# Moving the early scatters of a one-core decoder layer between the last steps of batches 14 and 15

## The reference

```python
x = layernorm(x + linear_attention(x))            # q softmax over 16 features, k softmax over tokens
x = layernorm(x + cross_attention(x, ctx, ctx))   # 16 heads of 16, scores 128x128 per head
probs = softmax(gelu(x @ wg1 + bg1) @ wg2)        # 8 experts per token
top_vals, top_idx = top_k(probs, 2)
h = gelu(einsum('nd,edh->enh', x, w_in))          # 512 hidden
o = einsum('enh,ehd->end', h, w_out)
x = layernorm(x + einsum('ne,end->nd', gates, o)) # gates: zero but for the two best
```

## Time and profile before

| what | value |
|---|---|
| median of 3 executions | 425.79 us (424.82 to 425.82) |
| the profiled execution, its own time | 424.05 us |
| its span, first to last instruction | 422.3 us |
| PE busy | 344.7 us, 82% |
| DVE busy | 308.2 us, 73% |
| ACT busy | 221.9 us, 53% |
| POOL busy | 218.0 us, 52% |

### The profile page before, as it was taken

One profiled execution on the slowest core, in us unless ns is written; L12 is line 12 of the kernel. 1 busy time (PEld: TensorE's weight loads), 2 busy tenths in 40 slices (PEclk: granted clock), 3 DMA queues, 4 the chain that ended last, 5 costly groups with the idle time before them and its releaser, 6 DMA issues. The chain is left out here.

```text
span 422.3 us, 12354 instructions
## 1 busy us (share of the span) xinstructions
PE 344.7 (82%) x4025; PEld 279.1 (66%) x4025; DVE 308.2 (73%) x912; ACT 221.9 (53%) x518; POOL 218.0 (52%) x287
## 2 busy tenths in 40 slices
PE   2977999999999999999888664688999999999100
PEld 1656777877778687776766343576899999988100
DVE  2866989888888888888887737378777655655193
ACT  3425666676766766667765236263545444343044
POOL 8344456765757657576547762633223333422173
PEclk9998999999999999999999885589999999999755
DMA  7610222210222112220012221416434322221493
GB/s 223 223 36 1 78 76 77 76 57 23 77 76 79 40 39 76 78 77 23 32 52 75 81 78 47 157 52 191 142 104 127 90 75 68 88 64 40 148 362 125
DMA packets 21387, 38.35 MB, mean 91 GB/s; under 512 B 3696, under 2 KB 11120, under 8 KB 21328
## 3 DMA queue, kind: packets, MB, share of 16 engines
q1 hardware_dynamic: 16768, 26.06, 19.7%
q0 software_dynamic: 3408, 9.41, 6.2%
q10 hardware_dynamic: 1152, 2.10, 1.3%
HBM read 24.71 MB, written 12.84 MB: 89 GB/s over the span
## 5 line engine op out<-in xcount | busy, mean ns | idle before, releaser
L586 POOL DMA_INDIRECT parts<-QKT,rows_all x39 | 37.6, 964 | 76.8 <-DVE QKT L1220 70.4
L328 PE MATMUL bank<-QS,EW 128*128 128x256 f16 (+1 forms) x384 | 61.7, 262 | 4.0 <-DVE XB L1033 2.6
L492 POOL TENSOR_TENSOR rstd<-veps,neghalf 128x1 f32<-128x1 f32 x48 | 38.7, 806 | 38.5 <-DVE veps L856 38.1
L1396 PE MATMUL bank<-EW,QV 128*128 x312 | 48.6, 273 | 1.4 <-DVE R L1212 0.5
L1212 DVE TENSOR_TENSOR R<-scratch,QV 128x512 f16<-128x512 f32 x39 | 26.8, 691 | 30.1 <-ACT scratch L776 18.4
L328 PE MATMUL bank<-XB,EW 128*128 128x256 f16 (+1 forms) x192 | 48.5, 261 | 0.0
L776 ACT ACTIVATE scratch<-bank 128x512 f32<-128x512 f32 x39 | 23.4, 600 | 39.2 <-PE bank L328 39.1
L328 PEld LDWEIGHTS bank<-QS,EW 128*128 x384 | 37.4, 101 | 10.0 <-issue 4.7
L1138 DVE TENSOR_REDUCE NM<-bank 128x4 bf16<-128x512 f32 x64 | 39.6, 679 | 2.8 <-PE bank L1551 2.5
L507 POOL DMA_INDIRECT bkt<-REC,dest x32 | 31.7, 989 | 18.5 <-DVE REC L898 8.6
L710 ACT ACTIVATE rows_all<-bank 128x512 f32<-128x512 f32 x64 | 33.2, 604 | 13.7 <-remote 6.9
(11 more groups left out here) (240 smaller groups left out, 938.4 us busy)
## 6 DMA issues: line engine op xcount, KB each, us to landing
scratch<-w_in SPq DMA_DIRECT2D x8, 512.0 KB, 3.8
scratch<-w_out SPq DMA_DIRECT2D x8, 512.0 KB, 3.3
rows_all<-bkt SPq DMA_DIRECT2D x15, 262.0 KB
XC<-x SPq DMA_DIRECT2D x16, 128.0 KB, 3.5
XC<-ctx SPq DMA_DIRECT2D x16, 128.0 KB, 3.3
EW<-parts SPq DMA_DIRECT2D x8, 256.0 KB, 6.7
EW<-parts ACTq DMA_DIRECT2D x8, 256.0 KB, 8.1
out<-rows_all SPq DMA_DIRECT2D x8, 256.0 KB, 2.1
```

The lines of the kernel that those rows point to most:

```text
L328: last = pe.matmul(dst, a(c), b(c), start=(c == 0 and i == 0), stop=(c == n - 1 and i == 2))
L492: pool.tensor_tensor(rstd[n][p][:], veps[n][p][:], neghalf[:, 0:1], ALU.pow).then_inc(s_rs[n], 1)
L586: pool.indirect_dma_start(parts, bass.IndirectOffsetOnAxis(ap=home[:, t, f:f + 1], axis=0), Y[t % 2][:, f, :], None).then_inc(s_put[t % 2] ...
L1396: last = pe.matmul(bank[4 + t % 2][:, f * D:(f + 1) * D], a[t % 2][:, h, f * P:(f + 1) * P], b[:, h, :], start=(h == 0 and i == 0 and f == 0),
```

## The change

Only POOL's list changes, in its tail. The scatters stay in the same order, all 32 of them, as do the powers. What moves is where they stand among the powers and the waiting steps.

```diff
-"pw1:15 sc:0 sc:1 x1b:15 sc:2 sc:3 past_mT:14 pw2:12 sc:4 sc:5 past_sc:14 sc:6 sc:7 past_nat:15 sc:8 pw2:13 sc:9 past_ex:14 sc:10 "
-"sc:11 past_mT:15 sc:12 sc:13 past_sc:15 sc:14 sc:15 pw2:14 sc:16 sc:17 past_pv:15 sc:18 pw2:15 sc:19 "
+"sc:0 pw1:15 sc:1 x1b:15 sc:2 sc:3 past_mT:14 pw2:12 sc:4 sc:5 past_sc:14 sc:6 sc:7 past_nat:15 sc:8 pw2:13 sc:9 sc:10 "
+"past_ex:15 sc:11 sc:12 pw2:14 sc:13 sc:14 past_pv:15 sc:15 sc:16 sc:17 pw2:15 sc:18 sc:19 "
 "sc:20 sc:21 sc:22 sc:23 sc:24 sc:25 sc:26 sc:27 sc:28 sc:29 sc:30 sc:31")
```

## The result

| | kernel before | kernel after |
|---|---|---|
| median of 20 executions each | 425.73 us (423.66 to 426.87) | 428.17 us (425.78 to 429.95) |
| the profiled execution, its own time | 424.05 us | 425.78 us |
| its span | 422.3 us | 424.0 us |

The change makes the kernel slower: ratio 1.0061, interval 1.0045 to 1.0078, which is 2.4 us. The forecast was 2.2 us the other way, and 428.17 us lies above the range.

The account below looks back on a forecast made before the run. It took the expert stage to be bound by PE and the drain by a chain of waits. Terms -2.3 and +0.1 gave -2.2 us, off the median of 425.79: 423.6 us, range 421.8 to 427.5.

Parts of the forecast that it names:

- Scatter 0 ahead of `pw1:15`: POOL's list: scatter 0, 1.25 us, fits the 2.50 us idle before the power; cost 0.1 us, ends 0 and 1.25.
- Late releases are made by scatters: Drain: scatters in the way make PE's scores seen late, 0.15, 1.76 or 4.08 us for batches 13, 14, 15.
- Batch 15's release at 1.76 us in place of 4.08: ACT's wait for batch 15's scores: with scatters 11 to 15 moved away, released as late as batch 14's; gain 2.3 us.
- PE's pause: PE's idle time before `ao2:14`: near 3 us in place of 5.18.
- the clock, priced at 0: PE at `ao2:14`: a shorter pause may keep 2.4 GHz, worth 0 to 0.9 us; taken as 0.
- The five scatters cost nothing: Between `pw2:14` and `pw2:15`: five scatters, not three, make `pw2:15` 0.5 us late, under a cover of 1.1 us; nothing.
- slower: the late release moves to batch 15's last product: Rival, chance 0.22: under five scatters over `pv:15` and `ao2:15`, a late release of 3.9 us gives 427.5 us.
- one of the signs named: Sign of being wrong: a "remote" or unexplained wait of 2 us or more between `pv:15` and `n2:15`.
- Two scatters behind `pw2:15` cost nothing: Scatters 18 and 19 before SP's first load: through at 260.35, ahead of `base` at 260.76; 0, at worst 0.5 us.
- the main term: Scatters 11 to 15 leave the wait for batch 15's scores: -2.3 us, bounds nothing and 3.93 us.
- the steps that I had priced at nothing: Waiting steps removed, scatters 11 and 12 ahead of `pw2:14`, five scatters between powers, two behind `pw2:15`: 0 each.
- the expert stage ends as much earlier as it starts: Expert stage, bound by PE and untouched by the change: all of an earlier start reaches its end.

Follow-up runs that it names:

- the fillers: Kernel after with twelve one-column memsets of an unused tile added on POOL ahead of `n2:11`; 424.95 us, 0.9985 (0.9956 to 1.0013) of the kernel before.
- the extra DMA: Kernel after with one more indirect DMA, of blank rows, issued on POOL ahead of `n2:11`; 414.35 us, 1.001 (0.9994 to 1.0025) of the kernel before.
- the rest alone: Kernel after with scatter 0 put back behind `pw1:15`; 413.57 us and, in another set, 425.38 us, each 0.9983 of the kernel before.
- the second run with none in the drain: Kernel before with scatters 0 to 19 moved behind `pw2:15` and the waiting steps among them removed, repeated in the third set; one execution of 440.15 us.
- the two halves: Kernel before with only scatter 0 moved ahead of `pw1:15`: 1.0048 and 1.0073; kernel after with scatter 0 back behind `pw1:15`: 0.9983 twice.
- the one run meant to tell it: Kernel after with scatter 0 behind `pw1:15` and two scatters, not five, between `pw2:14` and `pw2:15`; 415.55 us, 1.0041 of the kernel before.
- the rest with the hold on the scores: Kernel after with scatter 0 behind `pw1:15` and scatters held for batch 15's scores, not its exponentials; 412.74 us, 0.9976 of the kernel before.

## Why the prediction was wrong

**The step that failed** is "Scatter 0 ahead of `pw1:15`. [...] I take 0.1 us, with 0 and 1.25 as ends". It measured 2.0 and 2.8 us alone. I priced the scatter's own duration against the idle time ahead of the power. That the destinations are known in time was nearly right (221.32 after, 1.96 us ahead of `pw1:15`'s data at 223.28; a scatter of 1.22 that starts 0.98 us after its release takes 2.20, and with the fillers `n1:15` is 0.4 us later than before, for the 0.1 that I took). What I left out was the way in: the scatter had always been issued behind an instruction that had waited, and I never asked what that wait hid. It hid the fetch of a block of instructions, whose packet went by 2.0 us before `pw1:15`'s data was there. With scatter 0 first the packet goes by 1.1 us after the wait for the release is over, in all four profiles of that order without fillers or the extra DMA; why not during that wait, as it did during the other, is open. Nothing that was in the trace of before carries its price as a duration. The sign was to be had: two q14 packets within 3 us of the place where POOL's order was to change. The upper end of the range, 427.5, was built from another mechanism, and the time lies beyond it.

**Late releases are made by scatters:** right, at the level at which the kernel was profiled, and shown by one execution there without any in the drain.

**Batch 15's release at 1.76 us in place of 4.08:** right in kind; it measured 1.12 after, and 243.01 - 241.44 = 1.57 in the rest alone. But 4.08 was the largest of the four profiles with the old order (2.30 to 4.08, mean 3.10), so the term of 2.3 us was too large from the start: the means give 1.54. PE's pause was 2.22 and 2.67 (about 3 forecast), and the clock, priced at 0, gave back 0.8 to 0.95 at `ao2:14`.

**The five scatters cost nothing:** wrong. The cover of `pw2:15` held at 426 us (its start is 0.19 us after POOL's last work, with `veps` as the releaser), but it was the wrong cover to look at. `base` doesn't hang on `pw2:15` but on the copy of `gh:13` at line 625, and the way from `pv:15` to that copy grew by 1.45 us in the mean, by 2.56 in the kernel after. That is the mechanism of the rival "slower: the late release moves to batch 15's last product", smaller than the 3.9 us given it there, and it was one of the signs named. It isn't what made the kernel slower: the rest alone has it in part and is no slower. At 414 us the five scatters held `pw2:15` up by 1.9 us.

**Two scatters behind `pw2:15` cost nothing:** held by a hair. I took the last scatter's packets for its landing, 2.15 us; SP's load starts 3.56 to 3.71 us after that scatter's start where it decides, of which 1.15 are SP's own, as behind `base`, so that the landing is 2.4 to 2.6. (In the second run with none in the drain it was 4.65 us from start to load, so the landing isn't always that quick.) In the kernel after, `base` was the last: SP's list has no row for the scatters.

**Sum:** the main term, -2.3, came out at some -0.5 (medians) together with the steps that I had priced at nothing, and the +0.1 at +2.0 to +2.8. I forecast -2.2 us in all, and +2.4 was measured; the two halves measured alone give +1.5 to +2.3. What the new late releases cost is known only as the mean of few profiles above, since the one run meant to tell it fell on the other level. That the expert stage ends as much earlier as it starts can't be seen in single profiles, where it takes 159.4 to 162.0 us.

**A better version:** the rest with the hold on the scores is 0.9976 (0.9964 to 0.9988) of the kernel before, 1.1 us, at 414 us. At 426 us it wasn't timed; there the rest alone and the kernel after with twelve fillers are both at 0.998, which their intervals don't tell from no change.

## What to carry to other kernels

A wait often hides more than what it waits for: before moving an instruction ahead of a wait, look for what else goes by during it, packets on the engine's instruction queue among them. When an order changes around a blocking wait, a late start with "issue" as its releaser is a reason to look at that queue; some cheap instructions earlier in the stream show at once whether the place of the fetch is the cause. When an instruction waits for several things, look at each of its waits: `base` was done 5.28 us before the load where it is usually 1.15, and the list of SP's waits had the scatter in a line of its own. And before taking the lateness of one wait as the price of a change, read it in more than one execution: the 4.08 us were 2.30 to 4.08.

## What the runs showed of the hardware

- A fetch of POOL's instructions at scatter 0's wait: in four profiles the packet goes by 1.1 us after the wait is over and the scatter starts 2.0 to 2.3 us behind the packet, 3.1 to 3.4 us after its release, in place of 0.98 where twelve small instructions had moved the fetch ahead. The Trainium skill, page "Runtime: NRT & Kernel Launch", section "Instruction fetch mechanics", has the fetch "mostly hidden"; here it was hidden in the kernel before, and 2.0 us of it were in the open after the change.
- The same kernel takes 414 or 426 us depending on the set. At 426 us results of PE are seen up to 4 us late beside indirect scatters; at 414 us ACT's list of waits has none of that kind in the same stretch. The drain has half of the 12 us, the expert stage the other half; whether that half has the same cause wasn't tried.
